# Starting three expert tiles inside the attention's drain, and fetching the payload's residual rows from DRAM

## The chip, the cores and the metric

The program runs on one core of one Trainium2 chip. The time is the device time of one execution in microseconds (us); the median of three runs is given. Engines are named as the profile names them: PE is TensorE, DVE is VectorE, ACT is ScalarE, POOL is GpSimd, SP is SyncE, which here only issues DMAs. A "q" behind a name (SPq, DVEq) is that engine's sequencer. All arithmetic is float32.

## The reference

The input x has 16 x 256 tokens of 128 features. Four residual blocks follow one another, each applied to a layer norm of x:

```python
x = x + attn_a(layernorm(x))   # linear attention, 16 heads of 8, then a 512-wide MLP, inner layer norms
x = x + ffn(layernorm(x))      # attention over groups of 16 tokens (4 heads of 32), then a mixture of experts
x = x + attn_b(layernorm(x))   # attention without softmax, 16 heads of 64
x = x + ffn(layernorm(x))      # the same ffn, same weights

# the mixture of experts in ffn; y is the layer norm of x + attention
idx = argmax(y @ Wg.T)                          # 8 experts, one per token
moe[t] = relu(y[t] @ W1[idx] + b1[idx]) @ W2[idx] + b2[idx]
ffn = layer_norm(y + moe) * g2 + be2
```

## The kernel before

The 4096 tokens are 32 tiles of 128, handled as 16 pairs. Each engine has its own program, a list of stages in this order: block A (`attn_a`), `attention_block(0)`, `experts(0)`, the folding of the weights of `attn_b` and `block_b`, `attention_block(1)`, `experts(1)`. Within a stage `pipeline` calls a `body(i)`; `has(k)` is true while pair i-k exists, so a body does step k for the pair that came k bodies ago. The order of the code in a body is the order on that engine, and engines meet through semaphores only. After body 15 no new pair begins; bodies 16 and on are the stage's drain. Pairs are counted from 0, so the last is pair 15.

**Attention block.** For each pair: layer norm (statistics on DVE, `rstd` and `shift` on POOL, the scaling on ACT), the products for q, k and v, scores, softmax on DVE, and the probabilities `p_c`, which SP moves with four DMAs (L1132) into the block-diagonal tile `p_t`. PE multiplies them with v (L1228, "the attention product"), then the output projection (L1188). A second layer norm is written by ACT into the payload, `pay[..., 0:D]` (L1278). PE turns it (L1219) and computes the gate (L1179); DVE finds the best expert (`best`, `hot`), PE counts how many tokens went to each expert before (L1168, L1170, "the rank"), and DVE writes each token's place (`pos`, L1419). POOL scatters the pair to `sorted_dram`, sorted by expert, with two indirect DMAs (L1509). A payload row is the normed row, the residual row x + b2f (`pay[..., D:2*D]`), and the token's number. The residual half is added by POOL (L1502) for pairs 0 to 11 and by DVE (L1453) for pairs 12 to 15. There are `PAYS` = 5 payload slots, so slot p%5 can be refilled once the scatter of pair p-5 has landed (semaphores `sorted_`).

**Lists.** Which rows of `sorted_dram` an expert tile covers, and which expert owns it (`first_row`, `owner`), is worked out on DVE. The first `EARLY` = 10 tiles depend on pairs 0 to 8 only and are made in the drain (`early_list`, parts 1 to 9); the other 29 need all pairs (`other_list`, parts 0 to 9, placed in the first expert bodies). The semaphore `tabled` tells of both.

**Weight products.** In the first attention's drain PE also computes the last seven of the products that fold layer norm weights and biases into the experts' matrices (`hat_products`, L485, numbers 10 to 16 in `HATS_LATE`), and DVE (L504) or ACT copies them out. `hat_copies` must end before an expert's matrix is used.

**Experts.** 39 tiles of 128 rows. SP reads the expert's number and loads the rows into one of nine slots (L1584). In body i PE turns tile i (L1598), multiplies tile i-1 with the first matrix (L1608, into HA_ and HB_) and tile i-2 with the second (L1619, L1621). ACT copies the turned rows, applies relu to the first half and copies the next first matrix out of `we` (L1631); DVE applies relu to the second half (L1670), copies the second matrix (L1692), and does the final layer norm of tile i-3 (L1666 `stats`) and tile i-4 (`xout` L1687). POOL scatters the result. The body of the first tiles is peeled, so Python conditions on i can change it.

`spin` issues products whose result nobody reads (L155). Where an attention block ends and the experts begin, the PE programs simply follow one another: pair 15's rank, two products for the totals, then tile 0.

Between the stages x travels through DRAM: block A's SP stores each `xout` to `x1_dram` (L936), and attention 0 loads it as `xa` once all sixteen stores have landed (`a_done`). `block_b` and attention 1 do the same through `x3_dram`.

## Time and profile before

| what | value |
|---|---|
| median of three runs | 683.97 us (683.65 to 685.65) |
| profiled execution, its own time | 686.3 us |
| span of its instructions | 684.5 us |
| mean granted TensorE clock | 0.981 |
| busy: PE, DVE, ACT, POOL | 637.8, 483.9, 380.5, 398.7 us |

The profile is of one execution; between its span and its own time lie 1.8 us. Ends of matmuls are modelled, so a start of one row and the start of the next tell more than a duration. "[0.60 <-PE bank L485]" behind a row means that the engine was idle for 0.60 us before it, until the named instruction let it go on.

### The profile page before, as it was taken

What the parts mean: (1) busy time and instruction counts of PE and PEld (TensorE: products, weight loads), DVE (VectorE), ACT (ScalarE), POOL (GpSimd) and SP (SyncE); (2) the same over time, 40 slices, a digit from 0 to 9 for tenths busy, and PEclk for the clock granted to TensorE, in tenths of its full rate; (3) what the DMA queues carried; (4) which work ended last, traced back from release to release, by engine and by line L of the source; (5) the groups of instructions that cost most, each with busy time, mean ns of one, the idle gap of its engine ahead of it and who ended that gap; (6) DMA issues with size and microseconds to landing.
All of it is one profiled execution on the core that took longest, in us unless ns stands there. A gap on an engine that the chain in (4) does not pass through costs nothing.

```text
span 684.5 us, 19055 instructions
## 1 busy us (share of the span) xinstructions
PE 637.8 (93%) x5450; PEld 545.5 (80%) x5450; DVE 483.9 (71%) x2160; ACT 380.5 (56%) x974; POOL 398.7 (58%) x714
## 2 busy tenths in 40 slices
PE   8999999968999899999978999999699999999993
PEld 5899999836778679999975788787577877998993
DVE  2586777759999858888851333324899996887884
ACT  2587777648888435555523333330787864555550
POOL 5466668954688654767751121230548877467666
PEclk9999999989999989999999999999999999999997
DMA  4961001161122441232240000001312224332220
GB/s 126 325 234 30 17 25 33 36 203 27 44 74 88 168 134 54 85 85 78 59 133 7 24 17 24 15 23 49 109 31 73 78 92 119 83 85 76 81 69 21
DMA packets 57929, 53.63 MB, mean 78 GB/s; under 512 B 7707, under 2 KB 52164, under 8 KB 57532
## 3 DMA queue, kind: packets, MB, share of 16 engines
q1 hardware_dynamic: 51050, 36.19, 18.6%
q0 software_dynamic: 5568, 12.96, 5.5%
q10 hardware_dynamic: 1234, 3.55, 1.4%
q8 instruction: 37, 0.61, 0.4%
q14 instruction: 40, 0.33, 0.2%
HBM read 31.33 MB, written 19.83 MB: 75 GB/s over the span
## 4 chain that ended last, share of the span: by engine, by line
PE 44%; DVE 29%; issue 9%; POOL 8%; DVEq 4%; ACT 3%; DMA 2%; SPq 0%; POOLq 0%; ACTq 0%
PE wide L1794 4%; PE wide L1767 4%; DVE hid_f L1670 4%; PE wide L619 4%; PE bank L1780 4%; DVE stats L1666 3%; DVEq L1663 3%; POOL sorted_dram L1509 3%; POOL rstd L1495 3%; PE wide L155 2%; DVE late L1692 2%; PE bank L672 2%; PE wide L636 2%; PE wide L663 2%; PE wide L485 2%
## 5 line engine op out<-in xcount | busy, mean ns | idle before, releaser
L1608 PE MATMUL bank<-zt,late 128*128 128x128 f32 x624 | 92.8, 284 | 5.1 <-DVE hid_f L1670 4.7
L1608 PEld LDWEIGHTS bank<-zt,late 128*128 128x128 f32 x624 | 79.8, 191 | 11.9 <-DVE hid_f L1670 10.2
L1509 POOL DMA_INDIRECT sorted_dram<-rows_e,pos x64 | 66.0, 1031 | 26.1 <-issue 15.5
L1551 POOL TENSOR_TENSOR rstd<-var_e,half_neg 128x1 f32<-128x1 f32 x78 | 47.8, 613 | 43.3 <-DVE xout L1687 30.2
L1631 ACT ACTIVATE late<-we 128x512 f32 x80 | 50.5, 631 | 26.8 <-PE bank L1608 20.2
L1619 PE MATMUL wide<-late,hid_f 128*128 128x128 f32 x416 | 55.1, 275 | 1.1 <-DVE tmp L1675 1.1
L1619 PEld LDWEIGHTS wide<-late,hid_f 128*128 128x128 f32 x416 | 50.6, 192 | 1.4 <-issue 1.4
L1746 POOL TENSOR_TENSOR var_m<-mvs,eps 128x2 f32<-128x2 f32 x16 | 3.1, 194 | 79.5 <-DVE mvs L1847 79.5
L1851 DVE COPY late<-wide 128x1024 f32<-128x1024 f32 x16 | 19.6, 1225 | 39.0 <-PE wide L1794 39.0
L1558 POOL DMA_INDIRECT out<-xout,dest x39 | 40.6, 1041 | 10.4 <-issue 10.4
L1558 POOL DMA_INDIRECT x_dram<-xout,dest x39 | 40.5, 1039 | 8.1 <-issue 8.1
L1278 ACT ACTIVATE rows_e<-tmp,shift,rstd 128x128 f32<-128x128 f32 x64 | 28.1, 487 | 30.6 <-POOL shift L1497 30.6
L1638 ACT ACTIVATE zt<-bank 128x128 f32<-128x128 f32 x78 | 21.6, 277 | 41.7 <-PE bank L1598 39.9
L1495 POOL TENSOR_TENSOR rstd<-var_m,half_neg 128x2 f32<-128x2 f32 (+1 forms) x50 | 40.2, 804 | 4.3 <-DVE nmean L1380 0.9
L1492 POOL TENSOR_TENSOR var_m<-mvs,eps 128x2 f32<-128x2 f32 (+1 forms) x40 | 9.1, 228 | 56.6 <-DVE mvs L1442 26.5
L537 DVE BATCH_NORM_STATS2 stats<-xa 128x6 f32<-128x128 f32 (+1 forms) x128 | 29.4, 271 | 15.9 <-DMA xa<-x_dram 10.0
L1295 ACT ACTIVATE z<-xa,shift,rstd 128x128 f32<-128x128 f32 x64 | 28.0, 489 | 21.9 <-POOL shift L1497 21.9
L155 PE MATMUL wide<-ones 128*128 128x256 f32 x120 | 37.0, 447 | 3.2 <-DVE we L504 1.2
L1692 DVE COPY late<-we 128x640 f32 x78 | 38.2, 490 | 1.7 <-issue 1.7
L1670 DVE TENSOR_SCALAR hid_f<-bank 128x256 f32<-128x256 f32 x78 | 33.1, 425 | 6.7 <-issue 1.6
L1641 ACT ACTIVATE hid_f<-bank 128x256 f32<-128x256 f32 x78 | 29.9, 384 | 13.7 <-PE bank L1608 13.7
L1844 DVE TENSOR_TENSOR m_sb<-bank,bo 128x128 f32<-128x128 f32 x16 | 4.7, 292 | 39.2 <-PE bank L1780 39.2
(300 smaller groups left out, 1947.3 us busy)
## 6 DMA issues: line engine op xcount, KB each, us to landing
rows_e<-sorted_dram SPq DMA_DIRECT2D x78, 128.5 KB, 2.1
xa<-x_dram SPq DMA_DIRECT2D x9, 640.0 KB, 6.0
we<-L_ffn_W SPq DMA_DIRECT2D x16, 256.0 KB
x_dram<-xout SPq DMA_DIRECT2D x32, 128.0 KB, 1.8
early<-late SPq DMA_DIRECT2D x128, 32.0 KB
sorted_dram<-L_attn_a_x ACTq DMA_DIRECT2D x2, 1028.0 KB
rows_e<-L_ffn_b SPq DMA_DIRECT2D x1, 1024.0 KB
hid_f<-L_ffn_b ACTq DMA_DIRECT2D x1, 1024.0 KB
```

The costliest lines, as they stand in the source:

```text
L155: nc.tensor.matmul(to[:, 0:2 * P], ones[:, :], ones2, start=True, stop=True)
L537: last = nc.vector.bn_stats(stats[:, slot, at + n, :], x)
L1495: nc.gpsimd.tensor_tensor(rstd[:, c, w], var_m[:, c, w], half_neg[:, w], ALU.pow).then_inc(g["rstd"], 1)
L1509: nc.gpsimd.indirect_dma_start(sorted_dram[n][:, :], bass.IndirectOffsetOnAxis(ap=pos[:, p % 3, t:t + 1], axis=0), pay[:, p % PAYS, t, :], ...
L1551: nc.gpsimd.tensor_tensor(rstd[:, s % 3, 0:1], var_e[:, s % 3, :], half_neg[:, 0:1], ALU.pow).then_inc(g["rstd"], 1)
L1558: nc.gpsimd.indirect_dma_start(target, bass.IndirectOffsetOnAxis(ap=dest[:, c, :], axis=0), xout[:, c, 0, :], None, bounds_check=T - 1, oo ...
L1608: last = nc.tensor.matmul(to[:, (m % 2) * P:(m % 2 + 1) * P], we_t[:, c1, m * P:(m + 1) * P], zt[:, c1, 0, 0:P], start=True, stop=True)
L1619: nc.tensor.matmul(VB[c2][:, 0:P], hid_e[:, c2, m, :], we_t[:, c2, F + m * P:F + (m + 1) * P], start=(m == 0), stop=False)
L1631: nc.scalar.activation(we_t[:, c, 0:F], we[:, bass.ds(e, 1), 0:F].rearrange("p a n -> p (a n)"), ACT.Copy).then_inc(g["w1"], 1)
L1641: nc.scalar.activation(hid_e[:, c1, 0:2, :], HA_[:, 0:256].rearrange("p (m t) -> p m t", m=2), ACT.Relu).then_inc(g["relu_a"], 1)
L1670: nc.vector.tensor_scalar_max(hid_e[:, c1, 2:4, :], HB_[:, 0:256].rearrange("p (m t) -> p m t", m=2), 0.0).then_inc(g["relu_b"], 1)
L1692: nc.vector.tensor_copy(we_t[:, c, F:], we[:, bass.ds(e, 1), F:].rearrange("p a n -> p (a n)"))\
```

## The change

It has five parts.

1. The stages ahead write a second copy of x. In block A and in `block_b` DVE adds b2f to each pair's `xout` into a new tile `xb`, and SP stores it to `xb_dram` behind the store of x. `a_done` and `x3_done` now count both.
2. In the attention block POOL's and DVE's additions of b2f (L1502, L1453) are gone. SP fetches the residual rows of pair i into the payload slot in its body i, behind the four DMAs of `p_c`; before it, SP waits until the scatter of pair i-5 has landed. POOL waits for this load before the scatter.
3. The weight products come at another place and two to a body (`HATS_LATE`), and the parts of `early_list` are drawn together, so that the early list is complete in DVE's body 24 and not 26.
4. In the last bodies of the attention PE, ACT and DVE do the first steps of expert tiles 0, 1 and 2, where PE had `spin` products (in the first and second attention alike). The expert pipelines return at once for i < `AHEAD` = 3.
5. For expert tiles 2 to 8 ACT does the relu of the second half, and `other_list` is placed two parts to a body in bodies 3 to 7.

```diff
@@ attention_block, sync
+                    if i >= 3:
+                        sp.wait_ge(pay_in[c], PAIRS + uses(i - 3, 3, 16))
+                    if i >= PAYS:
+                        sp.wait_ge(sorted_[i % PAYS], uses(i - PAYS, PAYS, 32))
+                    sp.dma_start(pay[:, i % PAYS, :, D:2 * D], xb_rows[:, 2 * i:2 * i + 2, :]).then_inc(pay_in[c], 16)
@@ attention_block, tensor
                         if i == PAIRS + 7:
-                            spin(pe, AV, 3)
+                            hidden_tile(pe, n, 1)
+                            output_tile(pe, n, 0)
...
                         if i == PAIRS + 6:
-                            spin(pe, AV, 1)
+                            turn_tile(pe, n, 2)
...
+                    if n == 0 and i == PAIRS + 1:
+                        pe.wait_ge(g["v"], o + PAIRS)
+                    hat_products(pe, *hats_between(n, i))
                     if has(5):
...
                         if i == PAIRS + 5:
-                            spin(pe, AV, 3 if n else 1)
+                            pe.wait_ge(g["wo_kept"], o + PAIRS)
+                            turn_tile(pe, n, 0)
+                            turn_tile(pe, n, 1)
+                            hidden_tile(pe, n, 0)
@@ attention_block, scalar
+                    if i == PAIRS + 5:
+                        act.wait_ge(tabled, n * 4 + 2)
+                        if n == 0:
+                            act.wait_ge(hat_kept, N_F)
+                        first_matrix(act, n, 0, 0)
+                        rows_turned(act, n, 0)
+                        rows_turned(act, n, 1)
+                        first_matrix(act, n, 1, 1)
+                    if i == PAIRS + 6:
+                        relu_half(act, n, 0, "a")
+                        relu_half(act, n, 0, "b")
+                        rows_turned(act, n, 2)
+                        first_matrix(act, n, 2, 2)
+                        relu_half(act, n, 1, "a")
+                        relu_half(act, n, 1, "b")
+                        first_matrix(act, n, 3, 0)
@@ attention_block, vector
+                    if i == PAIRS + 11:
...
+                        second_matrix(dve, n, 0)
+                        second_matrix(dve, n, 1)
+                    if i == PAIRS + 12:
+                        second_matrix(dve, n, 2)
@@ experts
+                    if isinstance(i, int) and i < AHEAD:
+                        return
...
+                    if isinstance(i, int) and AHEAD <= i <= ACT_RELU:
+                        relu_half(act, n, i - 1, "b")
...
-                    if has(1):
+                    if has(1) and not (isinstance(i, int) and i <= ACT_RELU):
                         dve.wait_ge(g["hid_b"], o + i)
@@ block_b, vector (block A likewise)
+                        nc.vector.tensor_tensor(xb[:, c, :, :], xout[:, c, :, :], b2f_2, ALU.add).then_inc(xb_made, 1)
```

`turn_tile` is one transposition, `hidden_tile` the four products with the first matrix, `output_tile` the five with the second, `first_matrix` and `second_matrix` read the owner's number and copy the matrix, `rows_turned` copies the transposed rows.

PE at the end of the first attention, before: pair 15's turning (L1219), the ranks of pairs 14 and 15 (L1168, L1170), its gate (L1179), and the first product of the totals (L1244).

```order
L155 MATMUL wide<-ones 128x256
L1219 MATMUL bank0<-ident,rows_e 128x128 x2
L485 MATMUL bank2<-ident,late 128x512
L1168 MATMUL wide<-hot,lower 128x16
L1170 MATMUL wide<-gone,ones 128x16
L155 MATMUL wide<-ones 128x256
L1179 MATMUL wide<-wg,z0 128x8 x2
L482 MATMUL bank1<-ident,late 128x24
L155 MATMUL wide<-ones 128x256 x3
L1168 MATMUL wide<-hot,lower 128x16
L1170 MATMUL wide<-gone,ones 128x16
L1244 MATMUL wide<-gone,ones 128x8
```

The same stretch of the change, on PE (L1307 turning, L1250 and L1252 rank, L1261 gate, L1134, L1144, L1156 and L1158 expert tiles, L1329 totals):

```order
L1307 MATMUL bank0<-ident,rows_e 128x128 x2
L1250 MATMUL wide<-hot,lower 128x16
L1252 MATMUL wide<-gone,ones 128x16
L1134 MATMUL wide<-ident,rows_e 128x128
L1261 MATMUL wide<-wg,z0 128x8 x2
L1144 MATMUL bank1<-zt,late 128x128 x2
L1144 MATMUL bank2<-zt,late 128x128 x2
L1156 MATMUL bank3<-late,hid_f 128x128 x4
L1158 MATMUL bank3<-late,zt 128x128
L1250 MATMUL wide<-hot,lower 128x16
L1252 MATMUL wide<-gone,ones 128x16
L1329 MATMUL wide<-gone,ones 128x8
```

The weight products left this place for earlier bodies. The `spin` products are gone, and tile 2's turning and the products of tiles 1 and 0 stand ahead of pair 15's gate and rank.

DVE at the same place, before: the choice of pair 15's expert (L1425 to L1447), the last copy of a weight product, `hot`, `gone` and the place, then the first expert body.

```order
L1433 TENSOR_TENSOR seen<-wide,best 128x16
L1436 TENSOR_TENSOR seen<-seen,rank_w 128x16
L1447 TENSOR_REDUCE best<-seen 128x2
L504 SCALAR_TENSOR_TENSOR we<-rows_f,bank2 128x4x128
L1332 TENSOR_TENSOR hot<-rank_w,best 128x16
L1343 TENSOR_TENSOR gone<-gone,hot 128x8
L1408 TENSOR_TENSOR place<-wide,hot 128x16
L1419 TENSOR_REDUCE pos<-place 128x2
L1663 TENSOR_LOAD owner
L1663 ISA x2
L1692 ISA
```

The same stretch of the change, on DVE (L1561 the end of the choice, L1176 and L1177 the second matrices, L1432 `hot`):

```order
L1561 TENSOR_REDUCE best<-seen 128x2
L1176 TENSOR_LOAD owner
L1176 ISA x2
L1177 ISA
L1177 COPY late<-we 128x640
L1176 TENSOR_LOAD owner
L1176 ISA x2
L1177 ISA
L1177 COPY late<-we 128x640
L1432 TENSOR_TENSOR hot<-rank_w,best 128x16
L1443 TENSOR_TENSOR gone<-gone,hot 128x8
L1516 TENSOR_TENSOR place<-wide,hot 128x16
```

Two reads of an owner's number with two copies now stand between pair 15's choice and its `hot`, for which its rank on PE waits.

SP at the end of the first attention, in the change: the `p_c` DMAs (L1208), the loads of the residual rows (L1214), the three loads of `attn_b`'s weights (L1971), then the first expert tile's rows (L1681, L1682).

```order
L1208 DMA early<-late 32x256 [waits m_att,m_p_c]
L1208 DMA early<-late 32x256 x3
L1214 DMA rows_e<-xb0_dram 128x2x128 [waits m_sorted4,a_r2]
L1208 DMA early<-late 32x256 [waits m_att,m_p_c]
L1208 DMA early<-late 32x256 x3
L1214 DMA rows_e<-xb0_dram 128x2x128 [waits m_sorted0,a_xz]
L1971 DMA early<-L0_attn_b_Wq 128x1024 [waits m_s]
L1971 DMA early<-L0_attn_b_Wk 128x1024
L1971 DMA early<-L0_attn_b_Wv 128x1024
```

Before, the L1214 rows are absent: SP went from one pair's `p_c` to the next, and to the weights, with no wait for a scatter.

## Rows read from the trace of the kernel before

**Rows 1.** Busy time by stretch: us, engines with counts, clock, DMA share, GB/s

```profile
142.00:253.50 111.50, 99.40 (x996) 77.17 (x995) 93.55 (x486) 72.49 (x210) 72.02 (x132) 0.94 0.32 97
```

**Rows 2.** Chain that ended last, in the first attention's drain: start, us, what

```profile
249.73 2.86 PE wide L155 x6
```

**Rows 3.** Timelines of POOL and DVE: start, us, instruction, shapes

```profile
187.20 0.73 POOL L1502 TENSOR_TENSOR rows_e<-xa,b2f 128x256 f32<-128x256 f32 x1
...
187.41 0.56 DVE L1436 TENSOR_TENSOR seen<-seen,rank_w 128x16 f32<-128x16 f32 x1
...
213.13 0.20 DVE L1436 TENSOR_TENSOR seen<-seen,rank_w 128x16 f32<-128x16 f32 x1
```

**Rows 4.** Timeline of PE, second attention: attention products of pairs 3, 8 and 9

```profile
510.46 0.65 PE L1228 MATMUL wide<-early,late 128*32 128x128 f32 x16
...
536.64 0.65 PE L1228 MATMUL wide<-early,late 128*32 128x128 f32 x16
541.72 0.64 PE L1228 MATMUL wide<-early,late 128*32 128x128 f32 x16
```

**Rows 5.** Timelines of SP, POOL and PE, first attention, and the page's DMA issues

```profile
221.30 2.71 SPq L1132 DMA_DIRECT2D early<-late  x4
...
219.74 1.10 POOL L1509 DMA_INDIRECT sorted_dram<-rows_e,pos  x1 [0.30 <-issue]
...
228.06 0.64 PE L1228 MATMUL wide<-early,late 128*32 128x128 f32 x16
...
sorted_dram<-rows_e,pos POOLq DMA_INDIRECT x64, 3.0
```

**Rows 6.** First attention's last bodies: PE's busy time, timelines, landing of Wv

```profile
224.46:242.39 17.93, 15.92 (x137) 1.00 0.47 164
...
244.40 0.88 ACT L1278 ACTIVATE rows_e<-tmp,shift,rstd 128x128 f32<-128x128 f32 x2 [2.31 <-POOL shift L1497]
...
252.38 0.45 PE L1168 MATMUL wide<-hot,lower 128*128 128x16 f32 x2
...
233.15 0.43 SPq L1873 DMA_DIRECT2D early<-L_attn_b_Wv  x1
...
early<-L_attn_b_Wv SPq DMA_DIRECT2D x1, 512.0 KB, 8.3
```

**Rows 7.** Page's groups of ACT's copies; timelines of DVE and ACT at attentions' ends

```profile
L1631 ACT ACTIVATE late<-we 128x512 f32 x80 | 50.5, 631 | 26.8 <-PE bank L1608 20.2
...
L1638 ACT ACTIVATE zt<-bank 128x128 f32<-128x128 f32 x78 | 21.6, 277 | 41.7 <-PE bank L1598 39.9
...
575.23 0.88 ACT L1278 ACTIVATE rows_e<-tmp,shift,rstd 128x128 f32<-128x128 f32 x2 [2.15 <-POOL shift L1497]
...
254.38 0.49 DVE L1692 COPY late<-we 128x640 f32 x1 [0.85 <-issue]
```

**Rows 8.** First expert bodies: DVE by stretch, by line; PE's and DVE's timelines

```profile
253.35:276.62 23.27, 19.72 (x83) 1.00 0.24 67
...
L1670 DVE TENSOR_SCALAR hid_f<-bank 128x256 f32<-128x256 f32 x9 | 3.8, 425 | 1.1 <-issue 0.8
...
L1666 DVE BATCH_NORM_STATS2 stats<-wide 128x6 f32<-128x128 f32 x4 | 1.2, 296 | 0.9 <-PE bank L1621 0.4 <-issue 0.3 <-PE wide L1621 0.3
...
258.31 0.27 PE L1598 MATMUL bank<-ident,rows_e 128*128 128x128 f32 x1
...
260.43 0.27 PE L1598 MATMUL bank<-ident,rows_e 128*128 128x128 f32 x1
...
274.70 0.30 DVE L1666 BATCH_NORM_STATS2 stats<-bank 128x6 f32<-128x128 f32 x1 [0.42 <-issue]
```

**Rows 9.** End of block A: all engines by stretch, and DVE's timeline

```profile
118.00:134.00 16.00, 15.90 (x111) 14.06 (x109) 11.36 (x31) 10.76 (x26) 15.29 (x30) 1.00 0.15 42
...
137.11 0.69 DVE L504 SCALAR_TENSOR_TENSOR we<-rows_e,bank 128x512 f32<-128x512 f32 x1 [0.60 <-PE bank L485]
...
138.17 0.42 DVE L791 TENSOR_TENSOR xout<-tmp,early 128x256 f32<-128x256 f32 x1
```

More of the change, by code:

```diff
@@ L966, in build @@
             "qv", "kk", "q", "k", "kd", "v", "s", "own", "max", "centred", "exp", "sum", "prob", "p_c", "att", "att_t", "wo",
-            "wo_kept", "gate", "gate_read", "best", "seen", "gone0", "hot", "rank", "placed", "pos", "pay_x")}
+            "wo_kept", "gate", "gate_read", "best", "seen", "gone0", "hot", "rank", "placed", "pos")}
         p_in = [sem(f"m_p_in{k}") for k in range(3)]
@@ L973, in build @@
         M_BODIES = PAIRS + 9
-        PAY_X_BY_DVE, MEANS_BY_DVE = PAIRS - 4, PAIRS - 5
+        MEANS_BY_DVE = PAIRS - 5
         def clear_p(dve, hats):
@@ L1102, in other_list, with times @@
                                         ALU.mult).then_inc(r_step, 1)
+        e_s = {k: sem("e_" + k) for k in (
+            "turned", "zt", "w1", "w2", "hid_a", "hid_b", "relu_a", "relu_b", "v", "stats", "agg", "var",
+            "rstd", "tmp", "dest", "y")}
+        loaded = [sem(f"e_loaded{k}") for k in range(ZS)]
+        stored = [sem(f"e_stored{k}") for k in range(3)]
+        def times(k, slots, n):
+            return 16 * n * len(range(k, ET, slots))
+        TB, HA_, HB_ = bank[0], bank[1], bank[2]
@@ new lines, in build, with turn_tile, hidden_tile @@
+        VB = [bank[3], bank[4], bank[5]]
+        AHEAD, ACT_RELU = 3, 9
+        def turn_tile(pe, n, k):
+            pe.wait_ge(loaded[k], times(k, ZS, n) + 16)
+            nc.tensor.transpose(VB[k][:, 256:256 + P], zs(k)[:, 0:D], ident[:, :]).then_inc(e_s["turned"], 1)
+        def hidden_tile(pe, n, k):
+            g, o = e_s, n * ET
+            pe.wait_ge(g["zt"], o + k + 1)
+            pe.wait_ge(g["w1"], n + o + k + 1)
+            after(pe, g["relu_a"], o + k)
+            after(pe, g["relu_b"], o + k)
+            for m in range(FC):
+                to = HA_ if m < 2 else HB_
+                last = nc.tensor.matmul(to[:, (m % 2) * P:(m % 2 + 1) * P], we_t[:, k, m * P:(m + 1) * P],
+                                        zt[:, k, 0, 0:P], start=True, stop=True)
+                if m == 1:
+                    last.then_inc(g["hid_a"], 1)
+            last.then_inc(g["hid_b"], 1)
@@ new lines, in output_tile @@
+        def output_tile(pe, n, k):
+            g, o = e_s, n * ET
+            pe.wait_ge(g["relu_a"], o + k + 1)
+            pe.wait_ge(g["relu_b"], o + k + 1)
+            pe.wait_ge(g["w2"], o + k + 1)
+            for m in range(FC):
+                nc.tensor.matmul(VB[k][:, 0:P], hid_e[:, k, m, :], we_t[:, k, F + m * P:F + (m + 1) * P],
+                                 start=(m == 0), stop=False)
+            nc.tensor.matmul(VB[k][:, 0:P], zt[:, k, 0, 0:P], we_t[:, k, 2 * F:], start=False, stop=True).then_inc(g["v"], 1)
@@ new lines, in relu_half, with second_matrix @@
+        def relu_half(act, n, k, half):
+            src, first = (HA_, 0) if half == "a" else (HB_, 2)
+            act.wait_ge(e_s["hid_" + half], n * ET + k + 1)
+            nc.scalar.activation(hid_e[:, k % 3, first:first + 2, :], src[:, 0:256].rearrange("p (m t) -> p m t", m=2),
+                                 ACT.Relu).then_inc(e_s["relu_" + half], 1)
+        def second_matrix(dve, n, k):
+            e = dve.value_load(owner[0:1, bass.ds(k, 1)], min_val=0, max_val=E - 1)
+            nc.vector.tensor_copy(we_t[:, k, F:], we[:, bass.ds(e, 1), F:].rearrange("p a n -> p (a n)")).then_inc(e_s["w2"], 1)
@@ L1712, in stored_to @@
             def stored_to(k, count):
-                return count + 16 * len(range(k, PAIRS, 3))
+                return count + 32 * len(range(k, PAIRS, 3))
             DEPTH, FIRST = 4, 7
```

118 lines of the change are left out of this document (64 added, 54 removed).

## The prediction, made before the change was run

> **What bounds the kernel now.** I read the busy times by stretch first, then the chain of what ended last, then timelines. In the first attention no engine has much to spare: in its 111.5 us PE is busy for 99.4 and DVE for 93.6 [rows 1]. The chain moves through three states. In the full part it runs over DVE and POOL. In the drain it is a loop: one pair's gate, DVE's choice, the next pair's statistics, POOL, ACT, PE; and near the end it runs through `spin` products that compute nothing, 2.86 us of them in one piece [rows 2]. The experts then begin empty.
>
> **POOL's additions go away.** Where POOL's addition L1502 runs from 187.20 to 187.93, DVE's product `seen`, which reads two SBUF tiles, takes 0.56 us and ends at 187.97; alone it takes 0.20 [rows 3]. So DVE gets back up to 0.36 us a pair. How much of it counts is set by PE: from the attention product of pair 3 to that of pair 8 lie 26.18 us, 5.24 a pair, but the next comes after 5.08, and PE has no idle time in it [rows 4]. So at most 5 x 0.16 = 0.8 us, in each attention: **-1.6** (bounds 0 and -2.5, if the pairs behind go faster as well).
>
> The Trainium skill says the same of the rows ("SBUF — State Buffer", section "SBUF: two separate sides"): VectorE and GpSimd share a port pair, and an instruction with two SBUF inputs blocks against a GpSimd one that reads SBUF, for its whole length. By that rule the change also pays, since the new `xb` additions are of that kind. What it would cost is worked out from rows under block A.
>
> **SP's new load.** A pair's four `p_c` DMAs take SP 2.71 us. Now the load of the pair before stands ahead of them, and waits for a scatter. For the `p_c` of pair 13, issued from 221.30, that is the scatter of pair 7: second DMA at 219.74, landing 3.0 us after its issue, so 222.7, with its engine time up to 1 us more, 223.7. Then some 0.4 us for the load's own issue, 2.7 for the four, and their landing. No row tells that one: it lies between nothing and the 4.0 us from SP's last issue (224.01) to the product that needs the rows (228.06). I estimate 1.3 to 2, under the scatter's 3.0, since no descriptors have to be made by POOL. That gives 228.1 to 228.8 against 228.06 [rows 5]. So the hold uses up the slack and little more; POOL's scatter comes up to 0.7 us earlier without the addition. I take 0 and keep +3 for the range.
>
> **The first attention's drain.** From the rank of pair 9 (224.46) to that of pair 13 (242.39) are 17.93 us, PE busy for 15.92 [rows 6]. The change puts the weight products where PE waited. It does all seven here, where before it did five: +1.2, so PE comes to pair 13's rank after 17.1, 0.8 earlier. Then ACT: pair 15's scaling (L1278) began at 244.40. ACT was idle for 2.31 us ahead of that [rows 6]. Now two matrix copies (0.63 each), two row copies (0.28) and two reads of an owner's number (put at 0.35) stand there, 2.5 us. With the late start of the second row copy, which waits for PE, it begins at about 244.9, +0.5. From it to pair 15's rank at 252.38 are 7.98 us. Taken away: `spin` and the last two weight products. One piece of the former was 2.86 long [rows 2], but DVE's choice runs beside it; I put 2.9 for all of them. Added: two second-matrix copies ahead of `hot`, 0.49 each with their owner's reads, of which the first shows 0.85 us [rows 7]: 1.8 together, less the 0.69 of the weight copy that stood there. 244.9 + 7.98 - 2.9 + 1.1 = 251.1, **-1.3**. Against this stands that tile 0's rows queue behind `attn_b`'s weights: the last of these landed 8.3 us after its issue at 233.15, at 241.5. SP now issues them behind the landing of pair 10's scatter: three pairs of 4.5 us (17.93 by 4) behind pair 7's at 219.74, and 3.0 for the landing, 236.2. That is 3 us later, and they land at 244.5 [rows 5, 6]. PE's turning of tile 0 is due about 1 us behind pair 13's rank, at 242.7. If it waits until 244.5 or 245, the drain ends at 253, +0.6. I take the middle, **-0.4** (bounds -1.5 and +1.5).
>
> **The second attention's drain** has no weight products, and is paced by POOL's scatters, which stay. ACT was idle for 2.15 us ahead of pair 15's scaling at 575.23 [rows 7], where 2.5 us of work are put: +0.4. The two second-matrix copies ahead of `hot` are bare here: +1.8. The shorter wait at the gate gives back 0.4. **+1.8** (bounds +0.5, +2.5).
>
> **The experts' first bodies.** From the last `pos` (253.35) to the `stats` of body 10 (276.62) DVE takes 23.27 us, in the second half of the program likewise. In the change bodies 0, 1 and 2 are gone from it. What leaves DVE: nine relus (tiles 0 to 8) and two matrix copies, 0.42 and 0.49 by duration; since such instructions overlap by some 0.08 us, I count 9 x 0.34 + 2 x 0.40 = 3.9; the idle time ahead of relu and `stats`, 1.1 + 0.9 = 2.0, since nothing is left there that DVE would wait for. 23.27 - 5.9 = 17.4. Bodies 8 and 9 have no list: DVE took 1.92 (274.70 to 276.62), without relu 1.6, but PE needs 2.12 (258.31 to 260.43): +1.1 [rows 8]. A read of an owner's number more shows: +0.3. In all 18.8, **-4.5** for each expert stage, **-9.0** for both (bounds -6 and -11). The list is ready four bodies after the end instead of six, and tile 10 comes after seven, so it is no wait. ACT's load in these bodies is 0.63 + 0.28 + 2 x 0.42 + 0.35 = 2.1 us a tile, no more than PE's 2.12.
>
> **Block A and `block_b`.** From 118 to 134 us POOL is busy for 15.29 of 16 us, PE for 15.90, DVE for 11.36 [rows 9]. DVE has room for 16 additions of 0.42. But by what rows 3 showed, each holds POOL for 0.2 to 0.42, and POOL has 0.7 us free in four pairs: it can fall 1 us behind before the drain's end. At that end DVE's last rounds follow a wait of 0.60 us (L504, 137.11) and three `xb` lie ahead of the last `xout` (138.17): 3 x 0.42 - 0.60 = +0.7. Behind it `xb` itself and its store: +0.5, and attention 0 waits for both stores. **+1.2** (bounds +0.5, +2.5). In `block_b` DVE is mostly idle, so only the last addition and store count: **+0.5**.
>
> **The sum.** -1.6 - 0.4 + 1.8 - 9.0 + 1.2 + 0.5 = -7.5. The profiled execution took 686.3 us (span 684.5 and 1.8 around it), and would take 678.8; it stands 0.3% above the median of the runs, 683.97, so the median becomes **676.5**.
>
> **The rivals.**
>
> *The path of the last pair takes it back (18%).* Three tiles' work is put in front of pair 15 on PE, ACT and DVE. If the rows come late and the reads cost their full 0.85 each time, the drains cost +1.5 and +2.5 and more: -1.6 + 1.5 + 3.5 - 9.0 + 2.0 + 0.5 = -3.1, so about **681**. For it: the position of L1176 ahead of `hot`. Against: PE and ACT were idle there.
>
> *The experts gain less (12%).* DVE may be followed by ACT as the pace of bodies 3 to 9, with relu, two copies and a read at 2.0 us, or list parts may hold `stats`. With -2.5 a stage: **680.5**.
>
> *The payload's load holds up `p_c` (10%), the other side.* SP's L1214 waits for a scatter ahead of every `p_c` from pair 6 on, ten pairs in each attention. Each microsecond by which the scatter lands later than I read, beyond a slack of about 0.7 us, stands in front of L1228 and so in the chain. It decides from 1.1 us too late a pair: (1.1 - 0.7) x 20 = 8. At 1.5 us it gives +16 - 7.5, about **692**. For it: 228.1 to 228.8 against 228.06. Against: the scatters come sooner by POOL's 0.73, and pair 13 is the case where the earlier scatter landed latest.
>
> *More is gained (12%)*: everything at its better bound, also a shorter wait for the first output, gives **671**.
>
> **How the numbers follow.** My forecast, 674 to 679, has 46%, the others 18, 12, 10 and 12, and 2% remain for things that I have not seen. 674 to 679 is the likeliest case's own range. The range for 8 in 10 takes in the two cases near 681 and most of the better one: 671 to 683.5. About 0.3% (2 us) is what a measurement of this kernel tells from no change. Faster by more: 46 + 12 + 12 and most of the 18, 84%. Within: 6%. Slower: the load's case and a little, 10%.
>
> **What the profile would show.** The distance of L1316 (the attention product) at 5.1 us a pair in the full part, with no `seen` of 0.5 us. SP's L1214 ends before the next `p_c` is ready in most pairs, and no PE idle time ahead of L1316 that a DMA ends. PE's turning of tile 0 waits for rows in the first attention and not in the second. Pair 15's `hot` comes 1.8 us after its choice. From the last `pos` to body 10's `stats` 18 to 19 us, and ACT's relu of the second half. Between block A and attention 0 the load of `xa` begins 1.2 us later, with two stores ahead. I am wrong if L1316 waits for `p_in`, if DVE's bodies 3 to 7 stay at 3 us, or if block A's last pairs are paced by POOL.

## The result: slower, 1.009

| | median | runs | ratio to before, 95% interval |
|---|---|---|---|
| before | 684.81 us | 4 | |
| the change | 692.24 us (687.53 to 694.47) | 4 | 1.0094 (1.0061 to 1.0128) |

676.5 us was forecast. The change is slower by about 6 us by the ratio (the medians differ by 7.4), and its executions lie 7 us apart, where those of before lie 2.3 apart. The profiled one took 687.53 us at a mean granted clock of 0.970, the fastest of the four; the other three had mean granted clocks of 0.966, 0.963 and 0.958. Three executions that ran at mean clocks of 0.84, 0.55 and 0.39 (one each of the trials `spins2` and `pay_relu` and of the kernel before) are left out of every number below.

The page of the profiled execution: its span, the busy time of the engines, and the granted clock in 40 slices.

```profile
span 685.8 us, 19082 instructions
...
PE 635.2 (93%) x5418; PEld 546.1 (80%) x5418; DVE 485.0 (71%) x2166; ACT 386.7 (56%) x992; POOL 383.0 (56%) x690
...
PEclk9999999979999968999999999999999999999998
```

The mean clock is 0.970, before 0.981. The dip stands in slices 15 and 16, where the first attention ends: 6 and 8 tenths here, 8 and 9 before.

**The full part went as forecast.** Attention products of pairs 3, 8 and 9 in the second attention, the answer to [rows 4]:

```profile
512.76 0.64 PE L1316 MATMUL wide<-early,late 128*32 128x128 f32 x16
...
538.14 0.64 PE L1316 MATMUL wide<-early,late 128*32 128x128 f32 x16
543.21 0.65 PE L1316 MATMUL wide<-early,late 128*32 128x128 f32 x16
```

They lie 5.08 us apart, from the first on (25.38 us for five, 26.18 before), and DVE's `seen` takes 0.18 us on average.

**The first drain did not.** SP, PE and ACT at its end, first the SP queue, then PE, then ACT (start, us, instruction; in brackets the idle time before it and what ended it):

```profile
239.09 0.37 SPq L1214 DMA_DIRECT2D rows_e<-xb_dram  x1
239.50 0.47 SPq L1971 DMA_DIRECT2D early<-L_attn_b_Wq  x1
...
242.53 9.97 SPq L1682 DMA_DIRECT2D rows_e<-sorted_dram  x9
```

```profile
248.28 0.45 PE L1134 MATMUL bank<-ident,rows_e 128*128 128x128 f32 x1 [1.77 <-DMA rows_e<-sorted_dram]
...
251.10 0.69 PE L1307 MATMUL bank<-ident,rows_e 128*128 128x128 f32 x2
...
258.06 0.45 PE L1250 MATMUL wide<-hot,lower 128*128 128x16 f32 x2
```

```profile
248.98 0.28 ACT L1167 ACTIVATE zt<-wide 128x128 f32<-128x128 f32 x1
249.64 0.63 ACT L1162 ACTIVATE late<-we 128x512 f32 x1 [0.39 <-issue]
250.18 0.87 ACT L1363 ACTIVATE rows_e<-tmp,shift,rstd 128x128 f32<-128x128 f32 x2
```

The weights' loads are issued from 239.50 (I had 236.2), tile 0's rows come after them at 248.28, and ACT, which copies those turned rows before it scales pair 15, scales it at 250.18. From pair 15's attention product (240.72) to its `pos` (259.18) are 18.46 us; before, 15.64 (237.71 to 253.35). The windows of this stretch (us, PE, PEld, DVE, ACT, POOL busy with counts, granted clock, DMA share, GB/s):

```profile
246.00:250.00 4.00, 2.07 (x9) 1.69 (x9) 1.40 (x11) 1.48 (x4) 3.04 (x5) 0.50 0.81 267
250.00:254.00 4.00, 4.00 (x20) 3.78 (x20) 0.87 (x6) 2.55 (x8) 0.82 (x2) 0.50 0.68 187
254.00:258.00 4.00, 3.51 (x17) 3.25 (x16) 1.44 (x6) 1.73 (x4) 1.59 (x2) 0.50 0.24 81
258.00:262.00 4.00, 4.00 (x21) 4.00 (x20) 2.18 (x11) 0.84 (x3) 1.54 (x2) 0.50 0.05 16
262.00:266.00 4.00, 4.00 (x34) 4.00 (x33) 2.85 (x16) 2.68 (x7) 2.29 (x4) 0.88 0.14 49
```

0.50 is the lower of the two levels, 1.2 GHz. The clock fell while PE waited, and then real products ran at half speed: eight of a hidden layer (L1144) take 2.07 us here and 1.16 in the second attention. The kernel before had such a stretch too in its profile: it ran from 246 to 253 and held many `spin` products, those of [rows 2] among them; here it runs from 246 to 263.

**The experts' first bodies** gain, but less than forecast. Their stretch from `pos` to the `stats` of body 10, the answer to [rows 8], and one of PE's waits in it:

```profile
259.18:279.53 20.35, 18.89 (x149) 18.55 (x150) 16.18 (x72) 12.31 (x31) 11.38 (x14) 0.91 0.19 59
...
276.91 1.13 PE L1717 MATMUL wide<-late,hid_f 128*128 128x128 f32 x8 [0.91 <-DVE tmp L1770]
```

20.35 us here and 19.74 in the second half of the program; 23.27 before, 18.8 forecast.

### The profile page after: what moved, and what is told of

It is laid out like the page before. It is cut to its first block, busy times and chain, and to the rows that moved or that the text cites. A ratio compares the mean times of both kernels' runs of the same rounds, so it can differ in the third digit from the quotient of the medians.

```text
span 685.8 us, 19082 instructions
## 1 busy us (share of the span) xinstructions
PE 635.2 (93%) x5418; PEld 546.1 (80%) x5418; DVE 485.0 (71%) x2166; ACT 386.7 (56%) x992; POOL 383.0 (56%) x690
## 3 DMA queue, kind: packets, MB, share of 16 engines
q10 hardware_dynamic: 1234, 3.55, 1.5%
## 4 chain that ended last, share of the span: by engine, by line
PE 44%; DVE 24%; POOL 10%; issue 9%; DMA 4%; ACT 4%; DVEq 3%; SPq 1%; POOLq 0%; ACTq 0%
PE wide L1890 4%; PE wide L1863 4%; PE bank L1876 4%; PE wide L624 4%; POOL sorted_dram L1620 3%; DVE hid_f L1765 3%; DVE stats L1761 3%; POOL rstd L1611 3%; DVEq L1758 3%; DVE late L1787 2%; PE bank L677 2%; PE wide L668 2%; PE wide L488 2%; PE bank L1706 2%; PE wide L641 2%
## 5 line engine op out<-in xcount | busy, mean ns | idle before, releaser
L1706 PE MATMUL bank<-zt,late 128*128 128x128 f32 x592 | 86.6, 284 | 2.5 <-DVE hid_f L1765 2.4
L1706 PEld LDWEIGHTS bank<-zt,late 128*128 128x128 f32 x592 | 75.9, 193 | 7.0 <-DVE hid_f L1765 5.7
L1733 ACT ACTIVATE zt<-bank 128x128 f32<-128x128 f32 x72 | 20.0, 277 | 38.0 <-PE bank L1696 35.0
L1736 ACT ACTIVATE hid_f<-bank 128x256 f32<-128x256 f32 x74 | 28.4, 383 | 14.1 <-PE bank L1706 14.1
L1787 DVE COPY late<-we 128x640 f32 x72 | 35.1, 488 | 0.0
L1910 ACT ACTIVATE late<-wide 128x1024 f32<-128x1024 f32 x16 | 16.4, 1024 | 27.7 <-PE wide L1863 27.7
L156 PE MATMUL wide<-ones 128*128 128x256 f32 x88 | 27.6, 458 | 4.7 <-DVE we L507 2.3
L1876 PE MATMUL bank<-late,early 128*128 128x128 f32 x256 | 31.3, 275 | 0.7 <-DVE late L1947 0.7
```

The costliest lines, as they stand in the source:

```text
L1706: last = nc.tensor.matmul(to[:, (m % 2) * P:(m % 2 + 1) * P], we_t[:, c1, m * P:(m + 1) * P], zt[:, c1, 0, 0:P], start=True, stop=True)
L1736: nc.scalar.activation(hid_e[:, c1, 0:2, :], HA_[:, 0:256].rearrange("p (m t) -> p m t", m=2), ACT.Relu).then_inc(g["relu_a"], 1)
L1787: nc.vector.tensor_copy(we_t[:, c, F:], we[:, bass.ds(e, 1), F:].rearrange("p a n -> p (a n)"))\
L1876: last = nc.tensor.matmul(MB[:, 0:P], wb_t[:, 0, k, :], fac[:, c, k, :], start=(k == 0), stop=(k == HB // 2 - 1))
```

## The experiments

Each ratio is to runs of the kernel before made on the same chip beside the trial; 6 to 12 timed runs each. The trials were run in five groups (`again` to `both`; `spins2` to `tiles`; `relu_b`, `relu_dve` and `pay_relu`; the three from `no_spin`; the last three), so between groups only the ratios can be compared. "Drain" is the time from pair 15's attention product to its `pos`, "first bodies" that from there to body 10's `stats`, "clock" the mean of the runs' mean granted clocks (before: 0.981 or 0.982).

| trial | what | ratio (interval) | clock | drains | first bodies |
|---|---|---|---|---|---|
| again | the change | 1.0086 (1.0052 to 1.0121) | 0.967 | 17.99, 13.10 | 19.75, 19.75 |
| rows | weights' loads later | 1.0051 (1.0022 to 1.0079) | 0.965 | 16.25, 15.25 | 19.75, 20.78 |
| spins | 8 + 4 spins in | 1.0156 (1.0129 to 1.0184) | 0.969 | 18.30, 18.01 | 19.75, 20.23 |
| both | the two above | 1.0168 (1.0138 to 1.0198) | 0.967 | 18.39, 16.60 | 19.74, 19.74 |
| spins2 | 2 + 3 and 2 spins in | 1.0048 (1.0021 to 1.0074) | 0.972 | 17.10, 14.52 | 20.67, 20.32 |
| last | last pair first | 1.0054 (1.0036 to 1.0072) | 0.964 | 14.16, 12.56 | 23.38, 23.15 |
| payload | parts 1, 2 alone | 0.9990 (0.9965 to 1.0015) | 0.979 | 15.94, 11.17 | 24.72, 22.85 |
| tiles | parts 3 to 5 alone | 1.0025 (1.0004 to 1.0046) | 0.967 | 16.64, 15.54 | 19.39, 19.38 |
| relu_b | ACT's relu alone | 0.9933 (0.9916 to 0.9951) | 0.981 | 12.78, 11.34 | 20.21, 20.22 |
| relu_dve | change, relu on DVE | 1.0153 (1.0123 to 1.0184) | 0.965 | 18.24, 16.21 | 22.01, 21.86 |
| pay_relu | payload + relu | 0.9927 (0.9898 to 0.9955) | 0.981 | 12.74, 10.56 | 20.25, 20.59 |
| no_spin | the same, no spins | 1.0021 (1.0000 to 1.0042) | 0.961 | 13.85, 12.52 | 21.70, 22.32 |
| no_ahead | change without part 4 | 1.0024 (1.0006 to 1.0043) | 0.972 | 14.63, 10.56 | 21.60, 21.42 |
| no_ahead2 | the same, own semaphore | 1.0012 (0.9992 to 1.0032) | 0.973 | 14.17, 10.81 | 21.51, 22.00 |
| hats | pay_relu + weight products' places | 0.9951 (0.9924 to 0.9977) | 0.975 | 13.65, 10.56 | 20.25, 20.63 |
| other | pay_relu + two list parts a body | 0.9995 (0.9970 to 1.0020) | 0.977 | 12.75, 10.70 | 21.56, 21.78 |
| early | pay_relu + early list's places | 0.9930 (0.9901 to 0.9960) | 0.981 | 12.74, 10.59 | 20.26, 20.28 |

Drains and first bodies are those of the one profiled execution; before they are 15.64 and 11.04, and 23.27 and 23.25.

**The change again.** No edit.

> The change once more, unaltered, as the control of this chip. Both theories: 688 to 694 us, ratio 1.005 to 1.013. The clock theory also expects that executions differ by several us, and that the longer ones have the lower mean granted clock, since the stretch at 0.50 behind the first attention is of varying length.

As expected, 690.01 us. The six runs go from 684.68 us at clock 0.977 to 694.44 at 0.959. A line through the change's eleven runs falls by 4.9 us for each 0.01 of clock and passes 683 us at 0.981; a line through 118 runs of the kernel before has 685.0 us there. From this I estimate that at equal clock the change would be 2 us faster, and that the lost 0.015 costs it 7 us. It is an estimate: no run of the change reached 0.981 (the highest was 0.977), and the line shows that time and clock go together, not which of them drives the other. A further execution of the change had 691.17 us at 0.965:

> A further execution of the change, for its trace. Clock theory: what tells executions apart are stretches at the granted clock 0.50 at the ends of the two attentions, between 245 and 263 us and between 574 and 592 us; at mean clock 0.977 they were 10 us long together, at 0.970 they were 20. Each further us there costs some 0.4 us of time.

```profile
576.00:580.00 4.00, 3.09 (x22) 2.37 (x20) 1.72 (x13) 2.34 (x7) 2.39 (x5) 0.96 0.68 163
580.00:584.00 4.00, 2.65 (x19) 2.24 (x19) 1.63 (x8) 3.09 (x10) 1.81 (x3) 0.89 0.62 166
584.00:588.00 4.00, 3.86 (x19) 3.89 (x20) 1.09 (x5) 0.45 (x1) 0.88 (x1) 0.50 0.20 70
588.00:592.00 4.00, 4.00 (x20) 4.00 (x21) 2.35 (x12) 1.67 (x4) 2.70 (x3) 0.50 0.18 66
```

These are its windows at the end of the second attention. PE stood idle for 2.3 of the 8 us ahead, then came some 10 us at 0.50. In the trial `again` the same place stayed at 1.00, though PE stood idle for 2.4 of 8 us there too (572 to 580), with a drain of 13.10 us and not 16.20.

**The weights' loads behind the first expert rows.**

```diff
 # SP, experts(n)
+if n == 0 and isinstance(i, int) and i == AHEAD:
+    for m, w in enumerate(("Wq", "Wk", "Wv")):
+        sp.dma_start(wb_raw[:, m, :], b[w]).then_inc(wb_in, 16)
```

> The change with the three loads of the next weights issued behind the rows of expert tiles 0 to 2 instead of ahead of them. Rows theory: tile 0's rows land at about 245 instead of 248 us, PE's wait of 1.77 us for them goes, ACT's scaling of pair 15 begins at 247 and not at 250.18, and the time falls by 2.5 to 4 us, to 688 to 690, also if the clock still falls. If the clock alone is the cause and falls for the other gaps: 691 to 693. The second attention has no such loads and stays.

The ratio is 0.35% less than that of `again`, and the medians, 686.92 and 690.01 us, lie 3 us apart as expected, but the two intervals overlap. In the trace the lateness is real. Counted from pair 15's attention product (240.78), tile 0 is turned after 5.8 us and pair 15's rank comes after 15.5; in `again` (239.23) they came after 7.7 and 17.2, and the drain is 1.7 us shorter:

```profile
246.61 0.45 PE L1134 MATMUL bank<-ident,rows_e 128*128 128x128 f32 x1
...
256.27 0.29 PE L1250 MATMUL wide<-hot,lower 128*128 128x16 f32 x2
```

The clock still fell (0.50 in all of 248 to 252), and the loss against before stayed at 0.5%.

**Spin products back.** `spin(pe, AV, 8)` ahead of tile 0's turning and `spin(pe, AV, 4)` ahead of pair 14's; in a second form 3 and 2 in the first attention and `spin(pe, TT, 2)` ahead of pair 15's turning in the second.

> The change with spin products put back into the first attention's drain: four ahead of pair 14's turning, eight ahead of the turning of tile 0 (the eight in both attentions), some 0.22 us each at full clock. Clock theory: PE's idle time of 1.15 and 1.77 us there let the granted clock fall from about 246 us to 262 us, and real work runs at half speed in it; with the gaps filled the clock stays at 1.00 and the time falls by 4 to 6 us, to 685 to 688. Work theory (three tiles' work stands in front of pair 15 whatever the clock is): 691 to 694, since the spins only add to what stands there.

> Spin products back and the weights' loads behind the first rows, together. Clock and rows theory: full clock through the first drain and no wait for rows, 682 to 686, below the kernel before or level with it. Work theory: 690 or more.

> Fewer spin products than in the trial before, where a call of spin turned out as two records of 0.23 us, so that eight took 3.7 us: two ahead of pair 14's turning and three (1.4 us) ahead of tile 0's turning in the first attention, two (0.9 us) ahead of pair 15's turning in the second, each shorter than the idle time it stands in. Clock theory: mean clock up to 0.975 or more, 686 to 688. If spins do not hold the clock, or are not hidden: 690 to 693.

`spins`, at 695.16 us, came out above both expected ranges, and `both`, at 696.19, inside that of the work theory, so neither bears out the clock theory; beside `spins` the later loads of `both` gained nothing (1.0168 against 1.0156). One call's product is two records of 0.23 us, so eight were 3.7 us of bare delay: ACT's copy of the turned rows waited for PE in the second attention, and pair 15's scaling with it.

```profile
577.62 0.28 ACT L1167 ACTIVATE zt<-bank 128x128 f32<-128x128 f32 x1 [3.47 <-PE bank L1134]
...
579.19 0.86 ACT L1366 ACTIVATE rows_e<-tmp,shift,rstd 128x128 f32<-128x128 f32 x2
```

The fitting dose gave 1.0048, 0.4% under the change with overlapping intervals, and a clock of 0.972, between the two theories. So spins laid into this change give back little, and no run shows that filling PE's gaps would undo its loss.

**The last pair first.** ACT copies turned rows behind pair 15's scaling, PE takes tile 0's first products behind pair 15's gate and the rest behind its rank, DVE copies second matrices behind `pos`.

```diff
 # PE, body PAIRS + 6
 last.then_inc(g["gate"], 1)
+if i == PAIRS + 6:
+    turn_tile(pe, n, 0)
+    turn_tile(pe, n, 1)
+    hidden_tile(pe, n, 0)
+    turn_tile(pe, n, 2)
```

> The change with the last pair's steps first on each engine: ACT scales pair 15 ahead of copying the turned rows, PE turns pair 15 and computes its gate ahead of tiles 0 and 1, and its rank ahead of tile 1's hidden and tile 0's output products, DVE copies the second matrices behind hot and pos. Order theory (the tiles' work holds up pair 15): from the attention product of pair 15 to its pos 15.5 to 16.5 us and not 18.0 to 18.5 in the first attention, 11 to 12 and not 13 to 14 in the second, 3 to 5 us less in all, 685 to 688 us. If the low clock alone makes the drain long, these distances shrink by under 1 us, and the time stays at 690 to 692.

The drains came out near the expectation, 14.16 (15.5 to 16.5 expected) and 12.56. But the first bodies took 23.38 and 23.15 us, what before had. The tiles' work had only moved behind `pos`, and part of it ran at 0.50 (the mean over the two stretches is 0.88 and 0.89). In sum 0.3% under the change, which the intervals do not tell apart.

**Parts alone.**

> The kernel before with the payload's path alone (parts 1 and 2): DVE's additions behind block A and block_b, the second stores, SP's loads; the expert tiles, the lists and the weight products as before. From the profile of the change: start of the first attention 2.9 us later, full parts 0.8 us shorter each, second start 0 to 0.5 later, the mean granted clock as before (0.98). So +1.3 to +1.8 us over the kernel before, ratio 1.001 to 1.004. The rival, that SP's waits hold the attention products in the drains: over 1.006.

> The change without the payload's path: POOL and DVE add b2f as before, SP's loads and the second stores are gone; the three expert tiles, the lists and the weight products stay as in the change. If the loss lies in the drains and in the clock: no gain over before, ratio 1.002 to 1.007, mean clock under 0.975, executions that differ by over 5 us. If the payload's path carries the loss: 0.988 to 0.994.

> The kernel before with one piece of the change alone: ACT does the relu of the second half for tiles 0 to 8 (before its copy of the next first matrix), no tile begins inside the attention, lists and residual rows as before. DVE sheds 9 x 0.34 = 3.1 us in each experts stage, and from the last pos to the stats of body 10 it takes 20.5 to 21 us and not 23.27. Theory that DVE's own length paces these bodies: 2 to 3 us less in each stage, 679 to 681 us, ratio 0.991 to 0.994, with the clock as before. Theory that the list's chain or ACT paces them: 0.998 or more.

> The change with the second half's relu of tiles 2 to 8 on DVE again (undoes this piece alone). DVE gets 7 x 0.34 = 2.4 us more in each experts stage: 4 to 5 us longer, 694 to 696 us, ratio 1.014 to 1.018, the distance from the last pos to body 10's stats 22 and not 19.75. If PE or the list's chain paces these bodies: under 1.011.

The payload's path costs nothing and gains nothing that can be told (0.9990, a little under the expected 1.001 to 1.004). Parts 3 to 5 alone lose 0.25%, and the clock is as low as in the change. The two do not add up to the change: -0.1% and +0.25% apart, +0.9% together. ACT's relu is worth 4.6 us by itself and 4.6 the other way when undone. In the kernel with ACT's relu alone (`relu_b`) PE is busy without a gap from `pos` to body 10's `stats`:

```profile
251.22:271.43 20.21, 20.21 (x172) 19.45 (x172) 16.84 (x75) 15.43 (x40) 11.12 (x13) 1.00 0.34 94
```

So this one piece brings the first bodies from DVE's pace to PE's, 20.2 us. In the change, as `again` shows it, three tiles' first steps are already done there, and PE is busy for only 17.27 us; the stretch is just 0.5 us shorter all the same, because DVE's bodies set the pace again:

```profile
257.22:276.96 19.74, 17.27 (x148) 16.64 (x148) 16.20 (x72) 12.32 (x31) 11.41 (x14) 1.00 0.20 60
```

Some of the relu's gain is paid back behind body 10: at body 14's `stats` `relu_b` is ahead of before by 2.2 and 2.8 us, and the change by 3.5 in both stages.

**What the low clock costs, in unchanged code.** In `relu_b` the first drain is the code of the kernel before, yet it took 12.78 us and not 15.64. The difference is the clock: 0.50 from 246 to 253 us in the one execution, 1.00 in the other. One window and the six `spin` records of [rows 2] in each, first before, then `relu_b`:

```profile
248.00:252.00 4.00, 4.00 (x13) 3.30 (x13) 1.77 (x10) 0.19 (x1) 1.91 (x2) 0.50 0.79 209
...
249.66 2.93 PE L155 MATMUL wide<-ones 128*128 128x256 f32 x6
```

```profile
248.00:252.00 4.00, 3.89 (x25) 3.25 (x24) 2.02 (x10) 0.83 (x3) 1.92 (x2) 1.00 0.73 210
...
248.68 1.56 PE L155 MATMUL wide<-ones 128*128 128x256 f32 x6
```

From pair 15's scaling to its rank it takes 7.98 us in the first and 5.23 in the second. So the 15.64 that I compared with was itself a drain at the low clock.

**Payload's path and ACT's relu, and then without spins.**

```diff
-xb[:, i % 3, :, :]).then_inc(a_stored[i % 3], 16)
+xb[:, i % 3, :, :]).then_inc(xb_last if i >= PAIRS - 3 else a_stored[i % 3], 16)
```

> The payload's path, ACT's relu as in the trial beside it, and the stores of the last three pairs' second copies on a semaphore of their own, so that the load of x waits for the stores of x alone. The payload's path alone stood at 0.999. If the parts add up: relu -0.7%, the earlier load -0.1 to -0.2%: 0.989 to 0.993, 677 to 680 us, faster than both kernels. If the load of x is paced by something else than the second stores, the same as the trial beside it.

> The kernel of the trial with payload path, ACT's relu and the separate stores (0.9927), with all spin products of the attention drains left out and nothing put in their place. Clock theory: the mean granted clock falls from 0.98 to 0.975 or less, there are stretches at 0.50 at the end of the second attention too, and the time rises by 2 to 5 us, ratio 0.996 to 1.000. If the spins do not matter for the clock: 0.990 to 0.994 and 0.98.

0.9927, and 1.0021 without the spins (`-spin(pe, AV, 3 if n else 1)`, `-spin(pe, KB, 2)` and the others of the drains), more than the 0.996 to 1.000 expected: 0.9% of the time for products whose result nobody reads. This takes out more than the change does, which keeps `spin(pe, KB, 2)` in the second attention. The end of the second attention, with them and then without:

```profile
574.00:578.00 4.00, 3.99 (x33) 3.66 (x32) 2.73 (x14) 3.33 (x10) 1.93 (x2) 1.00 0.82 249
```

```profile
572.00:576.00 4.00, 1.80 (x10) 1.61 (x10) 2.65 (x21) 1.64 (x5) 3.04 (x5) 0.64 0.34 81
576.00:580.00 4.00, 2.65 (x13) 2.56 (x13) 1.41 (x9) 1.01 (x2) 2.70 (x4) 0.50 0.69 180
580.00:584.00 4.00, 4.00 (x16) 3.54 (x17) 2.19 (x12) 1.19 (x3) 2.74 (x3) 0.50 0.82 216
```

**The change without its tiles, and what lies between.** With `AHEAD = 0`, the tiles' steps taken out and the spins back:

> The change with its fourth part alone undone: no tile's step inside the attention, spin products where they stood before, the expert pipelines start at body 0; the payload's path, the places of the weight products and of the list's parts, two parts to a body, and ACT's relu for tiles 0 to 8 stay. If the tiles' steps inside the drain carry the loss: 678 to 681 us, ratio 0.990 to 0.994, mean clock 0.98. If the weight products' or the lists' places carry a part of it: 0.997 or more.

> As the first of this call, with the stores of the last three pairs' second copies on their own semaphore, so that the load of x waits for the stores of x alone. 0 to 1.5 us less than the first: ratio 0.988 to 0.993. This is the best version that the trials so far point to.

Part 4, the tiles' steps in and the spins out, carries 0.6%, but not all: 1.0024 is still 1% above 0.9927. `no_ahead2` missed its expectation (0.988 to 0.993), and its 1.0012 cannot be told from 1.0024. Three more trials put one of the remaining pieces each on the 0.9927 kernel:

```diff
 # other
-if i < 2:
+if i < 5:
     other_list(dve, n, 2 * i)
     other_list(dve, n, 2 * i + 1)
-elif i < 8:
-    other_list(dve, n, i + 2)
 # hats
-HATS_LATE = {PAIRS + 1: (10, 12), PAIRS + 2: (12, 13), PAIRS + 3: (13, 14), PAIRS + 4: (14, 15), PAIRS + 5: (15, 16),
-             PAIRS + 6: (16, 17)}
+HATS_LATE = {PAIRS + 1: (10, 12), PAIRS + 2: (12, 14), PAIRS + 3: (14, 16), PAIRS + 4: (16, 17)}
```

> The 0.9927 kernel (payload path, ACT's relu, separate stores; all else as before) with one piece more of the change: the weight products of the first drain at the change's places, two to a body and complete two bodies earlier. From the trace of the change without its tiles (clock 0.50 from 244 to 259 us, where the 0.9927 kernel kept 1.00): this piece takes away work that kept PE busy late in the drain, and should carry 3 to 4 of the 6 us between the two, ratio 0.997 to 0.999. If the lists' places carry them: 0.992 to 0.994.

> The 0.9927 kernel with the list of the other 29 tiles placed two parts to a body in bodies 0 to 4, as in the change, and not one to a body from body 2 on. The distance from the last pos to body 10's stats was 20.2 us without and 21.5 with it: 1.3 us in each experts stage, ratio 0.995 to 0.997. If that distance came of the clock in the first bodies: 0.992 to 0.994.

> The 0.9927 kernel with the early list's parts drawn together as in the change, complete in DVE's body 24. It moves a few small DVE operations from drain bodies with idle time into earlier ones: 0 to +1 us, ratio 0.992 to 0.995.

The shares were the other way round than I expected: `other` +0.7%, `hats` +0.2%, `early` nothing. Two list parts in one body make that DVE body 3.27 us long in the change (`stats` at 272.74 and 276.01), against PE's 2.12 a tile, and PE stops for a bank that DVE has not read; in `other`, at the same place of the queue:

```profile
265.94 1.13 PE L1634 MATMUL wide<-late,hid_f 128*128 128x128 f32 x8 [0.92 <-DVE tmp L1694]
```

`hats` takes from the late drain products that had kept PE busy: its clock is 0.975, and its profile has a low stretch from 244 to 252 us where `pay_relu` has none.

## Why the prediction was wrong

**The ledger**, each piece by the trials that differ in it (0.1% is 0.7 us): payload's path and ACT's relu together -0.7%, of which the relu is all but 0.1; two list parts a body +0.7%; the weight products' places +0.2%; the early list's 0; the load of x behind both stores +0.1%; three tiles inside the attention, with their spins out, +0.6%. The sum is +0.9%, as measured. Each piece holds its own share of the clock. 0.2 to 0.35% is the half width of most intervals here, so only the relu, the list parts and the tiles stand clear of them.

The pieces are not independent. Without the payload's path the same ledger gives -0.7 + 0.7 + 0.2 = +0.2% before the tiles, and `tiles` measured +0.25% with them. So, within these intervals, the tiles' 0.6% arises only together with the payload's path. The late rows are one thing that needs both: in `tiles` SP issues `attn_b`'s weights 5.0 us ahead of pair 15's attention product, in the change 1.2 us ahead. They account for 0.35% at most; the rest of this is open.

**Forecast and profile, term by term**, in the profiled execution of 687.53 us against that of before: start of the first attention +1.2 forecast, +2.9 measured; the payload's path inside the attentions -1.6, and -0.3; the first drain -0.4, and +2.8; the second +1.8, and +3.0; the first bodies -9.0, and -6.4; `block_b` and what lies around it +0.5, and -0.6. Forecast -7.5, measured +1.3. The median execution of the change took 4.7 us more than this one, and the slower ones have the lower clocks.

**The step that failed is the one on `spin`.** I wrote of the drain "Taken away: `spin` and the last two weight products ... I put 2.9 for all of them", and counted them as time gained. The 2.86 us of [rows 2] were six records at a granted clock of 0.50; at 1.00 the same six took 1.56. With every `spin` product in place the way from pair 15's scaling to its rank took 7.98 us at 0.50 and 5.23 at 1.00. The change has the tiles' products in place of `spin` in this drain, and took 7.88 us, at 0.50; the forecast was 7.98 - 2.9 + 1.1 = 6.2. So what I booked as the price of `spin` was the price of the low clock, and it stayed. None of my terms and none of my rivals has the granted clock in it, though the first attention's row showed it at 0.94 [rows 1].

That `spin` products buy clock was measured: without them 0.9927 turns into 1.0021, with the clock at 0.961. How much of the change's own loss comes of their absence was not isolated: part 4 takes them out and puts the tiles in, together +0.6%, and spins laid back gave 0.4% within overlapping intervals. The clock's 0.015 would cost 7 us by the line through the change's runs, about the whole loss, but that is the estimate from above. In the stretch around it, gaps of PE stay (waits for rows, for ACT and for DVE's choice), and behind them the tiles' products run at 1.2 GHz, in front of the last pair.

**The experts' -9.0 was mis-sized.** The first bodies took 19.75 us in the trial `again` and not 18.8, so -3.5 and not -4.5 a stage. The work leaving DVE was right: its busy time fell from 19.72 to 16.20 us, by 3.5 (3.9 forecast). The 2.0 us of idle time that I also took off did not go: DVE stood idle for 3.55 us of the stretch before and for 3.54 in the change. "If DVE's bodies 3 to 7 stay at 3 us" was my own sign of error, and they stayed at 2.9 to 3.4. I had costed the list's double parts at nothing; in `other` they cost 1.3 us at body 10 and 4.7 in all.

**The first drain: -0.4 forecast; +2.8 in the profile.** The mechanism was named (rows behind the weights, scaling of pair 15 behind them on ACT), its sizes were low. The weights were issued at 239.50 and not 236.2, but most of that is that the whole attention ran 3.0 us later (pair 15's product at 240.72, before 237.71). Counted from this product the rows let PE go on after 7.6 us and not 6.8, and ACT scaled pair 15 after 9.5 us and not 7.2. With the 1.7 us that the step on `spin` missed, this is about the gap between -1.3 and +2.8. "PE and ACT were idle there" held for time, not for clock.

**The second drain** was forecast at +1.8. Where the clock stayed at 1.00, in `again`, it was +2.06 (11.04 to 13.10): right. With low stretches it was +3.0 and +5.2 in the two other executions of the change that were profiled.

**The payload's path** was right in its parts. The full part runs at 5.08 a pair, and SP's loads hold up almost nothing: in the second attention PE waited 0.6 us in all for `p_c` rows, ahead of the last product. From pair 8's product to pair 15's it takes 34.20 and 32.66 us, 33.43 and 32.31 before, so the late pairs give back 0.8 and 0.35 of what the full part gained (0.65 and 0.8), and little is left of the -1.6. Block A's end was +1.2 forecast; the first `stats` came at 147.13 and not 144.23, +2.9 in this profile. Of it 1.6 is DVE's end (`xout` 139.80 against 138.17) and 1.3 the wait for the stores. In `pay_relu`, with the last stores on their own semaphore, 3.89 us lie between the last x store's issue and the load and not 4.64.

**The rivals.** The one on this side of the sign was the wrong one: SP's load did not hold up `p_c`. What came true were the mechanisms of two others together, each of which I had priced alone and as still faster: the last pair's path (+1.5 and +3.5 in the drains and +2.0 in block A there, +2.8, +3.0 and +2.9 in the profile) and list parts that hold up the experts (-2.5 a stage there, -2.9 and -3.5). That they exclude one another was my assumption. The granted clock, with which the rest of the loss goes, stood in none of the four cases.

**The best version found** is the payload's path with ACT's relu, everything else as before: 0.9927 (0.9898 to 0.9955), a median of 678.2 us. ACT's relu alone on the kernel before, 679.99 us and 0.9933, cannot be told from it, and is the smaller edit; nor can `early`, 0.9930.

**Open.** Why some executions of one kernel lose more clock than others is not settled, only where: the profiled ones show it at both attentions' ends. Open too is why the tiles cost 0.6% with the payload's path and next to nothing without it, and what share the missing spins have in that. Whether the tiles inside the attention would pay with one list part a body and more of PE's gaps filled was not tried.

## What to carry to other kernels

Before taking filler products out of a drain, read the granted clock of that stretch and of the next, and cost the real work behind them at both levels; filling PE's gaps with work that itself waits for a DMA or for another engine was no substitute here. The price of an instruction read from one profile holds for the clock of that profile: read the clock beside it. Measure a bundled change piece by piece, and in more than one order: here one piece was worth -0.7% and three others undid it, one of them only in company. When work is moved off the engine that paces a stage, look up at once who paces it next: with ACT's relu PE had no gap in 20.2 us, and with PE's work cut to 17.3 us the stretch still took 19.75, since DVE's list parts had been doubled up.

## What was not expected of the hardware

The time and the mean granted clock of single executions of one kernel go together closely: 684.68 us at 0.977 to 694.44 at 0.959, and in the kernel before, over 118 runs, 3.9 us for each 0.01. The same drain code took 15.64 us in an execution that stood at 0.50 for 7 us of it, and 12.78 in one that stayed at 1.00. PE had been idle for 1 to 2 us at a time before the clock fell, and in another execution it had been idle as long at the same place and the clock stayed (580 to 592 us in one execution, not at all in another). Once at 0.50, stretches with PE busy in 4.00 of 4.00 us, 250 to 254 and 258 to 262, were still at 0.50.
